# Counts per expert and row places: taken from VectorE and given to GpSimd, for seven of eight batches

## What is computed

```
x = x + tanh(g_xattn) * attention(layernorm(x), ctx, ctx, encoding, Wq, bq, Wk, bk, Wv, bv, Wm, bm)
h = layernorm(x)
top_logits, top_idx = top_k(h @ gate_w, 2);  w = softmax(top_logits)
out = sum over e of  w[e] * ((silu(h @ w0[e]) * (h @ w1[e])) @ wo[e])
x = x + tanh(g_ffn) * out
```

## Time and profile before

| | us |
|---|---|
| median of 3 runs | 1248.05 |
| lowest and highest | 1248.02, 1255.01 |
| the profiled execution, its own time | 1250.65 |
| its span, first to last instruction | 1248.8 |
| PE busy in the span | 1108.2 (89%) |
| DVE busy | 810.6 (65%) |
| ACT busy | 684.1 (55%) |
| POOL busy | 351.4 (28%) |
| mean granted TensorE clock | 0.933 |

### The profile page before, as it was taken

How to read it: one execution, slowest core, us unless ns; L and a number is a source line. 1 busy time by engine, 2 the same in 40 slices (tenths; PEclk the granted TensorE clock), 3 DMA queues, 4 the chain that set the end, 5 groups by cost and what they waited for, 6 DMA issues and landing times.

```text
span 1248.8 us, 17279 instructions
## 1 busy us (share of the span) xinstructions
PE 1108.2 (89%) x5417; PEld 441.9 (35%) x5417; DVE 810.6 (65%) x1603; ACT 684.1 (55%) x932; POOL 351.4 (28%) x371
## 2 busy tenths in 40 slices
PE   3548898998989898998854999999999999999996
PEld 1102233332323233332231444444444444444442
DVE  6757787777777787878545556565636565563631
ACT  2136776776767676776723446464626464462521
POOL 3154554647374654410111011111101111110101
PEclk9659998999999999988676999999999999999999
DMA  5653341223131313122164557686747676574443
GB/s 172 203 202 130 115 145 64 76 67 103 38 125 44 112 61 112 54 71 71 63 237 147 129 137 200 141 199 143 195 74 202 140 201 138 135 197 74 68 60 59
DMA packets 189652, 153.07 MB, mean 123 GB/s; under 512 B 130176, under 2 KB 150656, under 8 KB 189568
## 3 DMA queue, kind: packets, MB, share of 16 engines
q1 hardware_dynamic: 179664, 132.26, 36.6%
q0 software_dynamic: 7744, 18.09, 7.9%
q10 hardware_dynamic: 2160, 1.68, 0.5%
HBM read 73.28 MB, written 41.75 MB: 92 GB/s over the span
## 4 chain that ended last, share of the span: by engine, by line
PE 72%; ACT 9%; issue 7%; DVE 5%; POOL 1%; DMA 1%; SPq 0%; POOLq 0%; ACTq 0%; DVEq 0%
PE psum L1083 30%; PE psum L1093 15%; PE psum L324 7%; ACT wh L429 6%; PE psum L313 6%; PE psum L214 5%; PE psum L255 3%; PE psum L301 2%; PE psum L223 2%; DVE MX L596 2%; PE psum L273 2%; ACT wh L386 1%; ACT Xr L422 1%; PE psum L237 1%; DVE CS L700 0%
## 5 line engine op out<-in xcount | busy, mean ns | idle before, releaser
L1083 PE MATMUL psum<-wh,xT 128*128 128x512 f16 x1728 | 382.8, 382 | 16.6 <-DVE xT L1165 16.6
L596 DVE TENSOR_REDUCE MX<-psum 128x2 f32<-128x1024 f32 x256 | 311.3, 1221 | 104.9 <-PE psum L301 101.1
L429 ACT ACTIVATE wh<-psum,es 128x512 f32<-128x512 f32 x512 | 321.2, 688 | 91.6 <-PE psum L313 90.1
L1083 PEld LDWEIGHTS psum<-wh,xT 128*128 128x128 f16 x1728 | 169.9, 98 | 223.5 <-issue 22.3
L1093 PE MATMUL psum<-wh,hT 128*128 128x512 f16 x864 | 194.0, 381 | 3.5 <-DMA hT<-hn 3.5
L313 PE MATMUL psum<-stg 50*128 50x512 f16 x512 | 150.9, 410 | 42.6 <-ACT wh L429 23.3
L1197 DVE TENSOR_TENSOR hh<-sg,psum 128x512 f32<-128x512 f32 x72 | 49.4, 686 | 159.4 <-ACT sg L1114 159.4
L1247 POOL DMA_INDIRECT out<-yb,target x36 | 56.2, 1562 | 338.9 <-ACT yb L1124 338.9
L324 PE MATMUL psum<-wh,vT 128*32 128x512 f32 x1024 | 148.7, 656 | 0.0
L301 PE MATMUL psum<-stg 48*128 48x512 f16 x512 | 119.7, 403 | 13.8 <-DVE MX L596 9.6
L493 DVE SCALAR_TENSOR_TENSOR wh<-stg,scw,wh 128x1024 f16<-128x1024 f32 x96 | 118.7, 1294 | 18.3 <-ACT wh L486 18.2
(11 more groups left out here) (180 smaller groups left out, 1009.2 us busy)
## 6 DMA issues: line engine op xcount, KB each, us to landing
stg<-in_w SPq DMA_DIRECT2D x16, 2048.0 KB, 10.2
stg<-in_wo SPq DMA_DIRECT2D x8, 2048.0 KB, 10.2
stg<-scr SPq DMA_DIRECT2D x192, 64.0 KB
Xs<-zero SPq DMA_DIRECT2D x40, 264.0 KB, 2.7
wh<-wh SPq DMA_DIRECT2D x64, 128.0 KB, 2.1
scr<-wh SPq DMA_DIRECT2D x32, 256.0 KB, 2.3
xs<-in_x SPq DMA_DIRECT2D x8, 512.0 KB, 5.3
out<-xs SPq DMA_DIRECT2D x8, 512.0 KB, 3.1
```

The lines of the kernel that those rows point to most:

```text
L429: act.activation(m.Pb[:, c % 2, hh, :], m.psT[tile % 2], ACT.Exp, scale=m.es[:, min(hb // 2, 2):min(hb // 2, 2) + 1]).then_inc(S["exped"], 1)
L596: dve.tensor_reduce(m.MX[:, hb % 2, c0:c0 + 9:8], m.psS[tile % 2], AX_X, ALU.max, negate=True).then_inc(S["maxed"], 1)
L1083: last = pe.matmul(m.psum[:, 2 * j + w, :], m.xT[:, 4 * xp + k, :], m.wh[(e % 2, w)][:, wp, c:c + 512], start=(k == 0 and xp == 0 and wp = ...
```

## The change

For the batches 0 to 6 the two additions to the counts and the computation of the places go from VectorE to GpSimd, behind `rows_lower` and ahead of the batch's scatter. The reduction over eight experts (one instruction on VectorE) is made of three additions that halve the width. For the last batch VectorE keeps both. Semaphores are split accordingly: `counted` and `placed` are now raised by GpSimd, `count_zero`, `last_counted` and `last_placed` by VectorE.

```
     def rank(b):
         pe.wait_ge(S["chosen"], b + 1)
-        pe.wait_ge(S["counted"], b + 1)
+        pe.wait_ge(S["count_zero"], 1)
+        if b:
+            pe.wait_ge(S["counted"], b)
...
     def choose(b):
...
         if b:
-            dve.wait_ge(S["ranked"], b)
+            dve.wait_ge(S["counted"], b)
...
     def ranked(b):
         dve.wait_ge(S["ranked"], b + 1)
         empties(dve.tensor_copy(m.RK[:, 2 * b:2 * b + 2, :], ...), S, ("r", b))
-        dve.wait_ge(S["counted"], b + 1)
-        step(dve.tensor_tensor(m.CS[:, :], m.CS[:, :], m.SEL[:, 0, :], ALU.add))
-        dve.tensor_tensor(m.CS[:, :], m.CS[:, :], m.SEL[:, 1, :], ALU.add).then_inc(S["counted"], 1)
+        if b == NB - 1:
+            dve.wait_ge(S["counted"], b)
+            step(dve.tensor_tensor(m.CS[:, :], m.CS[:, :], m.SEL[:, 0, :], ALU.add))
+            dve.tensor_tensor(m.CS[:, :], m.CS[:, :], m.SEL[:, 1, :], ALU.add).then_inc(S["last_counted"], 1)
 
     def places(b):
         v = slice(2 * b, 2 * b + 2)
         evacuated(dve, S, ("r", b))
+        dve.wait_ge(S["placed"], b)
...
-        dve.tensor_copy(m.POS[:, v, :], m.POSF[:, :, :]).then_inc(S["placed"], 1)
+        dve.tensor_copy(m.POS[:, v, :], m.POSF[:, :, :]).then_inc(S["last_placed"], 1)
...
-            if s == 14:
+            if s == 14 and b == NB - 1:
                 places(b)
...
+    def count(b):
+        evacuated(pool, S, ("r", b))
+        pool.wait_ge(S["chosen"], b + 1)
+        pool.wait_ge(S["count_zero"], 1)
+        step(pool.tensor_tensor(m.CS[:, :], m.CS[:, :], m.SEL[:, 0, :], ALU.add))
+        pool.tensor_tensor(m.CS[:, :], m.CS[:, :], m.SEL[:, 1, :], ALU.add).then_inc(S["counted"], 1)
+        pool.wait_ge(S["counted"], b + 1)
+
+    def places(b):
+        v = slice(2 * b, 2 * b + 2)
+        PM = m.PM
+        step(pool.tensor_tensor(m.PF[:, :, :], m.RK[:, v, :], m.eb[:, :]..., ALU.add))
+        step(pool.tensor_tensor(PM[:, :, :, :], m.OH[:, v], m.PF[:, :, :]..., ALU.mult))
+        step(pool.tensor_tensor(PM[:, :, :, 0:4], PM[:, :, :, 0:4], PM[:, :, :, 4:8], ALU.add))
+        step(pool.tensor_tensor(PM[:, :, :, 0:2], PM[:, :, :, 0:2], PM[:, :, :, 2:4], ALU.add))
+        step(pool.tensor_tensor(m.POSF[:, :, :], PM[:, :, :, 0], PM[:, :, :, 1], ALU.add))
+        pool.tensor_copy(m.POS[:, v, :], m.POSF[:, :, :]).then_inc(S["placed"], 1)
+
     def scatter(b):
-        pool.wait_ge(S["placed"], b + 1)
+        if b < NB - 1:
+            pool.wait_ge(S["placed"], b + 1)
+        else:
+            pool.wait_ge(S["last_placed"], 1)
...
                 rows_lower(pool, m, S, (ph - 3) // 2)
                 pool.wait_ge(S["rows_lower"], (ph - 3) // 2 + 1)
+            if ph < LAST:
+                count((ph - 3) // 2)
+                places((ph - 3) // 2)
             scatter((ph - 3) // 2)
...
 def tensor_experts(pe, m, S, nc):
-    pe.wait_ge(S["counted"], NB + 1)
+    pe.wait_ge(S["last_counted"], 1)
```

More of the change, by code:

```diff
@@ L809, in vector_attention @@
     dve.memset(m.epst[:, :], EPS).then_inc(S["eps"], 1)
-    dve.memset(m.CS[:, :], 0.0).then_inc(S["counted"], 1)
+    dve.memset(m.CS[:, :], 0.0).then_inc(S["count_zero"], 1)
     step(dve.memset(m.zero[:, :], 0.0))
@@ L879, in x1_root @@
         pool.wait_ge(S["x1_root"], b + 1)
+    def count(b):
[8 more added lines that the diff above has]
+        PM = m.PM
+        step(pool.tensor_tensor(m.PF[:, :, :], m.RK[:, v, :], m.eb[:, :].rearrange("p (o e) -> p o e", o=1).to_broadcast([128, 2, 8]), ALU.add))
+        step(pool.tensor_tensor(PM[:, :, :, :], m.OH[:, v], m.PF[:, :, :].rearrange("p i (o e) -> p i o e", o=1).to_broadcast([128, 2, 2, 8]), ALU.mult))
+        step(pool.tensor_tensor(PM[:, :, :, 0:4], PM[:, :, :, 0:4], PM[:, :, :, 4:8], ALU.add))
+        step(pool.tensor_tensor(PM[:, :, :, 0:2], PM[:, :, :, 0:2], PM[:, :, :, 2:4], ALU.add))
+        step(pool.tensor_tensor(m.POSF[:, :, :], PM[:, :, :, 0], PM[:, :, :, 1], ALU.add))
+        pool.tensor_copy(m.POS[:, v, :], m.POSF[:, :, :]).then_inc(S["placed"], 1)
     def scatter(b):
-        pool.wait_ge(S["placed"], b + 1)
+        if b < NB - 1:
+            pool.wait_ge(S["placed"], b + 1)
+        else:
+            pool.wait_ge(S["last_placed"], 1)
         pool.wait_ge(S["filled"], 16 * NE * LEAST)
```

## The result

The changed kernel takes 1234.11 us (median of 4 runs, 1228.02 to 1235.72) against 1250.19 us (median of 4 runs, 1248.02 to 1255.01): a ratio of 0.9857, 95% interval 0.9809 to 0.9905. The profiled execution took 1232.96 us with a span of 1231.1 us, so 17.7 us less span than before.

What follows compares the result with a forecast made beforehand. The prediction took VectorE's lateness with `ON` at five phase ends, where TensorE waits, as the bound the change removes. 12.0 (idle time) + 8.0 (clock) - 1.5 (L603) = 18.5 us less than 1248.05: 1229.5 us, range 1223 to 1238.

Steps and rivals of the forecast that it cites:

- The idle time: Ends of phases 3, 5, 7, 9, 11: TensorE's 2.4 us waits for VectorE's `ON` all vanish, 12.0 us.
- The clock: Even phases behind the five waits keep full clock and last as long as phase 2: 8.0 us, at most 10.6.
- Rival (a): Clock falls at those phases' starts anyway, or L603 takes back its gain: only 10.5 us less, 1237.5; chance 0.17.
- L603's block: VectorE, slot 15: L603 now sits blocked by GpSimd's L551; costs 0.3 us a place, 1.5 in all, at most 8.0.
- GpSimd, 2.4 us and free: Eight small instructions added behind `rows_lower` take 2.4 us a batch and cost 0, since GpSimd has idle time.
- the room of 5.2 us: GpSimd ahead of the Newton iteration: the eight added instructions cost something only beyond 5.2 us.
- rival (b): GpSimd becomes late: beyond 8.2 us of room, 2.6 us a batch come back, giving 1242.5; chance 0.07.
- b = 5 and 6 at nothing: Last two batches moved, without such a wait: removing the six VectorE instructions gains nothing, at most 2.2 us in all.
- rival (c): Slower: the eight GpSimd instructions wait for VectorE's port or take 1.75 us each, 14.6 us a batch; 1261.5, chance 0.03.

Runs made afterwards that it cites:

- delay_six: The changed kernel with six 128x512 reductions on VectorE ahead of the `n` job of slot 14, for b = 0 to 4: 1256.17 us, 1.0051.
- vector_next_phase: The kernel before, all work on VectorE, counts and places moved to slot 2 of the next, even phase: 1232.83 us, 0.9871.
- unblocked: The kernel before, with GpSimd waiting for the batch's places ahead of `rows_lower`; no work changes engine: 1235.07 us, 0.9899.
- again: The changed kernel once more, unaltered, timed in a second set of 6 runs against the kernel before: 1228.22 us, 0.9838.
- rows_last: The changed kernel with counts and places on GpSimd ahead of `rows_lower` rather than behind it: 1230.77 us, 0.9859.
- counts_only: The kernel before with only the counts moved to GpSimd; the places stay on VectorE in slot 14: 1248.16 us, 0.9996.
- places_only: The kernel before with only the places moved to GpSimd; the two count additions stay on VectorE in slot 13: 1240.5 us, 0.9912.
- order_on_vector: The kernel before, all work on VectorE, counts and places called behind the jobs of slot 14 rather than ahead: 1241.89 us, 0.9946.
- thin_before: The kernel before with logits from the first 128 of 512 channels only, so tokens go to other experts: 1260.79 us, 1.009.

## Why the prediction was right

The forecast was 1229.5 us with a range of 1223 to 1238; 1234.11 and 1228.22 were measured. The mechanism was right for the phase ends and the even phases. That the sum is as near as this is in part luck. Point by point:

- **The idle time of 5 x 2.4 = 12.0 us** was right in place and size: no wait for `ON`, odd phases at full clock 33.03 against 35.50. `delay_six` and `vector_next_phase` show that it was VectorE's lateness there, and `unblocked` that the block beside L551 was its larger part (1.6 of 2.4 us).
- **The clock, 8.0 us** by the even phases, was right for all five of them (31.42 us for a forecast of 31.41, and 1.33 less in phase 12). Its upper bound of 10.6 was put too high: the slow stretches, taken as 3.8 and 6 us, last 3.4 and 6.1, which makes 9.9. But the term was wrong as a net: I took the odd phases for unaffected. A fall there costs 0.8 or 2.4 us. In the profiled execution phases 5 to 11 gave back 3 x 0.85 + 2.4 = 5.0 us; in `again` the same four gave back 2.4 + 0.8 + 0.8 = 4.0. Rival (a), that the clock falls all the same, was wrong for the start of the even phases and true elsewhere, at 5.0 and 4.0 us against 8.0. (In the chances, two thirds of (a) were put on the fast side of 1235.6, though its own figure, 1237.5, lies behind that border.)
- **L603's block, 1.5 us**, was forecast as a block of 1.6 us and measured as 1.53 (1.70 less 0.17). `rows_last` shows a price of zero, so this term of the sum was 1.5 us too much.
- **GpSimd, 2.4 us and free**, was right: 2.2 us, and GpSimd still idles 2.7 to 3.1 us ahead of the Newton iteration, where I had 2.8. That agrees with the room of 5.2 us, though no run tried a load between 2.2 and 9 us. With 24 more instructions (9 us) GpSimd had no idle time left there, and the first cost was blocked VectorE instructions; with 40 it was the SP queue, which I had not looked at. By rival (b)'s rule, with 40 more, 13.4 us less 8.2, a batch would lose 5.2; it lost 4.8, though at another place.
- **b = 5 and 6 at nothing, with 2.2 us as the upper end.** Here the forecast missed a term: phases 13 to 17 are 4.7 us shorter in the profile after and 6.4 in `again`. From phase 12 to the experts TensorE spent 77.3 us at half clock before and 59.8 and 56.2 after. This stage has long idle times in both kernels, and I looked at its waits but not at its clock. Two causes suggest themselves, and the other profiles bear out neither alone. The six instructions gone: phase 13 lasts 30.12 us at clock 1.00 in `counts_only`, where the places are still on VectorE, and 34.00 at 0.85 in `delay_six`, where all six are gone at this place. A phase 12 without a fall: `places_only` and `unblocked` have that, and their phase 13 lasts 33.96 and 34.09. So the cause stays open, and part of the term may be scatter of the clock that has nothing to do with the change.

So the sum came out near because errors of opposite signs met. In the profiled execution 12.0 + 8.0 us were right, 5.0 were lost again in the odd phases, 4.7 came on top in phases 13 to 17, the 1.5 for L603 were not lost, and ahead of phase 4 only 0.4 us were gained where the first of the five idle times alone was worth 2.4.

## What to carry to other kernels

Look at the durations of tiny VectorE instructions: one that takes 0.7 to 2 us, where its like takes 0.2, and ends with a GpSimd instruction is blocked by it. Before moving work from one engine to the other, try moving either of the two in time (one wait added here gained 14 us). Such a block costs in full ahead of the instruction that others wait for. Behind it, it was free on L605 in slot 15, but cost 1.3 us a place in `order_on_vector`, where the next row maxima stood behind it. A fall of the clock that is removed at one place may turn up at another stretch, so take the clock of all phases into the sum, not that of the one repaired.

## What the runs showed of the hardware

A fall of the granted clock lasted 3.4 or 6.8 us at half speed in phases 4 to 11 of every profile. One of 3.4 cost 1.33 us in an even phase and 0.8 in an odd one, one of 6.8 cost 2.4 in an odd one; half speed for 3.4 us is 1.7 us of work, so part of it was covered, and by what was not looked into. Waits of 0.8 us at a phase's end had no fall behind them in 5 of 5 even phases (`unblocked`), and those of 2.3 to 3.1 us had one in 16 of 19 (the kernel before, `delay_six`, `counts_only`, `thin_before`). The SBUF — State Buffer page of the Trainium skill (section Who interferes with whom) says that issue order decides who blocks. By that rule, the runs agree as far as they go: in `counts_only` the same cast took 1.92 us where it started behind GpSimd's 2.1 us instruction (L553), and 0.80 where it started behind L361 and ended with it, ahead of L553. In both cases GpSimd's instruction had come first. The opposite order stands in the profile of the changed kernel once, at b = 6 (one row each of VectorE's and GpSimd's timeline):

```profile
605.98 1.28 DVE L495 SCALAR_TENSOR_TENSOR wh<-stg,scw,wh 128x1024 f16<-128x1024 f32 x1
606.20 1.12 POOL L890 TENSOR_TENSOR CS<-CS,SEL 128x8 f16<-128x8 f16 x1 [3.60 <-issue]
```

VectorE's instruction has started first and ends at 607.26; the small addition on GpSimd behind it ends at 607.32 and takes 1.12 us instead of the 0.23 of b = 0. The prediction's argument against rival (c), that only GpSimd takes the port, thus holds for its rows but not in general; it cost 0.9 us once, beside the 14.6 that (c) needs in each batch.
